# A graph attention layer: the radial network per pair of tiles on quarters of the array, one row load per pair, sums stored only where a node block ends

## The chip, the cores and the metric

One core of one Trainium2 chip runs the kernel. The metric is device time in microseconds, median of several runs. The kernel before takes 6380.22 us (three runs, 6365.9 to 6386.08).

## The reference

One attention layer over a graph of 12500 nodes with 128 features and 400000 edges, sorted by destination. Cut to what matters:

```
h       = relu(layernorm(x))
message = (h @ w_src + b_src)[src] + (h @ w_dst)[dst]
rad     = silu(silu(edge_attr @ w1 + b1) @ w2 + b2) @ w3 + b3     # 32 -> 64 -> 64 -> 128
message = message * edge_weight * rad
msg_h   = (message @ w_sep + b_sep) as 8 heads of 16 alpha + 16 value
score   = sum(smooth_leaky_relu(alpha) * alpha_dot) per head
att     = softmax of score over the edges of one dst
out     = x + segment_sum(value * att, dst) @ w_proj + b_proj
```

## The kernel before

Nodes are cut into 98 blocks of 128. Edges, in order of destination, are cut into chunks of 256. An item is a chunk with one node block that it touches; two items make a tile of 512 edges, sixteen tiles a group. There are 1664 items, 832 tiles and 52 groups. A first stage (to about 250 us) works out node features and tables, among them the rows of places (each edge's node within its block, rel_rows) and of edge weights (ea_rows). A last stage (from about 6290 us) divides and projects. The edge stage between them is written out completely: each engine has its own `step(g, j)` for tile t = 16 g + j, all in one fixed order, tied by semaphores only.

In step t:

- SP loads for tile t + 3 the transposed attributes (attr, 32 KB per item), the two windows of destination rows (win, 128 KB per item, only if the block has changed in that slot), the places (rel_bc, L986) and the edge weights (ea_bc, L987), both one row broadcast to 128 partitions. Which block an item belongs to is worked out in SP's registers from packed words (`steer_to`). Then it stores the running sums of tile t - 29 (L1005). At j = 14 it also loads the group's masks in ten transfers. Four buffers each.
- GpSimd gathers source rows, four indirect DMAs of 128 rows per tile (L1047), let go when the transposes of tile t - 4 are done.
- PE (TensorE): transposes of the gathered rows into xT_ps (L1337); z1 of tile t + 1 (L1256); the aggregation of tile t - 28 (L1297); every fourth step the scores (L1307); softmax odds and ends; then, when the message is there, alpha (a_ps, L1353), z2 of t + 1 (L1262), values (v_ps, L1358), radial of t + 1 (L1271, two row halves), destination part of t + 1 (L1284). Every f32 matmul is two instructions, an f32r one and a transpose are one.
- VectorE: message of tile t, xT_ps times rads (L1159); `weigh` of t - 27: one-hot places (hot, L1123) and weighted values (wval, L1129); `accumulate` of t - 28: two steps of the running sum with the aggregation (L1146, L1149), into one of four buffers that must have been stored; a piece of the softmax; the smooth leaky ReLU (L1169); rads of t + 1 (L1115), which reads radial's PSUM.
- ScalarE: first Silu of t + 1 (L1184), copy of the values (L1204), Silu of alpha (L1231), second Silu of t + 1 (L1190), places to a one-hot by distance (L1196, L1198) for t + 2, the copy of a tile's weights (L1211).

Radial's output takes half of each of two PSUM banks (rad_ps); the aggregation writes beside it. The softmax's small products have a bank of their own (misc_ps).

Of the kernel before, what the change touches and what calls it, by code (L numbers as in the profile page):

```python
# [4 lines left out]
P = 128  # L5
# [4 lines left out]
CE = 2 * P  # L10
TE = 2 * CE
# [3 lines left out]
LAG = 28  # L15
# [47 lines left out]
def gnn_kernel(nc, x, src, dst, edge_attr, edge_weight, w_src, b_src, w_dst, fc_w1, fc_b1, fc_w2, fc_b2,  # L63
# [32 lines left out]
    rel_rows = dram("rel_rows", (NI, CE), bf16)  # L96
    ea_rows = dram("ea_rows", (NI, CE))
# [6 lines left out]
    with ctx:  # L104
# [27 lines left out]
        z_ps = ctx.enter_context(nc.psum_tensor("z_ps", [P, 512], f32))  # L132
# [4 lines left out]
        misc_ps = ctx.enter_context(nc.psum_tensor("misc_ps", [P, 512], f32))  # L137
        rad_ps = ctx.enter_context(nc.psum_tensor("rad_ps", [P, 2, 512], f32))
        PS = [v[:, :] for v in (z_ps, xT_ps, a_ps, v_ps, sc_ps, misc_ps)] + [rad_ps[:, 0], rad_ps[:, 1]]
# [15 lines left out]
        with ExitStack() as part, nc.Block() as block:  # L155
# [10 lines left out]
            count_ps = misc_ps  # L166
# [250 lines left out]
        with ExitStack() as part, nc.Block() as block:  # L417
# [79 lines left out]
            def _(sp):  # L497
# [24 lines left out]
                def store_rows(k):  # L522
# [3 lines left out]
                    sp.dma_start(ea_rows[rows, :], ea_g[:, u]).then_inc(s_out[u], 16)  # L526
# [3 lines left out]
                    sp.dma_start(rel_rows[rows, :], rel_b[:, u]).then_inc(s_out[u], 16)  # L530
# [335 lines left out]
        with ExitStack() as part, nc.Block() as block:  # L866
# [7 lines left out]
            attr = tb("attr", [P, U, P])  # L874
            win = tb("win", [P, U, 2, PARTS, C], f32r)
            rel_bc = tb("rel_bc", [P, U, TE], bf16)
            ea_bc = tb("ea_bc", [P, U, TE])
            idx = tb("idx", [P, 2, 2 * G], i32)
            gath = tb("gath", [P, U, SUB, C])
            hotT = tb("hotT", [P, 2, TE], f32r)  # L880
            apart = tb("apart", [P, 2, TE])
            row_below = tb("row_below", [P, 1])
            h1 = tb("h1", [P, 2, CE])
            h2 = tb("h2", [P, 2, CE])
            rads = tb("rads", [P, 2, TE])
# [3 lines left out]
            hot = tb("hot", [P, 2, SUB, P])  # L889
            wval = tb("wval", [P, 2, SUB, H, HV])  # L890
# [21 lines left out]
            s_attr = [ts(f"attr_in{u}") for u in range(U)]  # L912
            s_win = [ts(f"window_in{u}") for u in range(U)]
            s_ea = [ts(f"edge_weight_in{u}") for u in range(U)]
            s_gath = [ts(f"gathered{u}") for u in range(U)]
            s_idx = [ts(f"indices_in{n}") for n in range(2)]
            s_rst = [ts(f"run_stored{r}") for r in range(R)]
# [27 lines left out]
            def _(sp):  # L945
                at = {}
                held = {}

                def steer_to(g, j):

                    half = j % (G // 2)
                    if half == 0 or j == AHEAD:
# [15 lines left out]
                def load(g, j, attr_v):  # L968
                    t = G * g + j
                    u = j % U  # L970
                    items = steer_to(g, j)
                    need(sp, s_z1, t - U + 1)
                    for i, (c, b) in enumerate(items):
                        sp.dma_start(attr[2 * RAD * i:2 * RAD * (i + 1), u], attr_v[bass.ds(c, 1)].rearrange("o f e -> (o f) e")).then_inc(s_attr[u], 16)
# [32 lines left out]
                def stepper(attr_v):  # L1007
                    def step(g, j):
                        t = G * g + j
                        if there(t + AHEAD):  # L1010
                            load(*later(g, j, AHEAD), attr_v)
# [9 lines left out]
                        if there(t - LAG - 1):  # L1021
                            store(*later(g, j, -LAG - 1))
# [535 lines left out]
```

## Time and profile before

| | |
|---|---|
| median of 3 runs | 6380.22 us |
| the profiled execution | 6405.65 us |
| its span | 6403.9 us |
| mean granted TensorE clock | 0.944 |
| PE busy | 5329.2 us, 83% |
| VectorE (DVE) busy | 3944.8 us, 62% |
| GpSimd (POOL) busy | 3635.5 us, 57% |
| ScalarE (ACT) busy | 3145.8 us, 49% |
| moved by DMA | 905.74 MB |

The profile is of one execution. Busy shares are means over stages. A matmul's end is modelled, while the moment at which an engine that waited for it starts is recorded. "remote" as a releaser is a signal that the profile gives to no instruction. PEclk is the granted clock of TensorE as a share of 2.4 GHz.

### The profile page before, as it was taken

To read this page: it belongs to the slowest core of one execution; us is meant where nothing else is said; L and a number is where in the kernel's file an instruction comes from. 1 tells how busy PE (TensorE), PEld (TensorE's weight loads), DVE (VectorE), ACT (ScalarE), POOL (GpSimd) and SP (SyncE) were. 2 spreads that over 40 slices of the span, in tenths; PEclk is the share of its full clock that TensorE was granted. 3 is DMA by queue.
4 is the path that set the end of the run, shared out by engine and by line. 5 is a ranking of instruction groups with operands and counts; after the bars stand their busy time and mean duration, and the time that the engine had idled before them with its cause. 6 is when DMAs were issued, how large, how long until landed. Compare 5 with 4: busy or idle time off the path is not lost. (4 is left out here: it accounts for less than half of the span.)

```text
span 6403.9 us, 120739 instructions
## 1 busy us (share of the span) xinstructions
PE 5329.2 (83%) x33155; PEld 4049.4 (63%) x33155; DVE 3944.8 (62%) x7812; ACT 3145.8 (49%) x6435; POOL 3635.5 (57%) x3491
## 2 busy tenths in 40 slices
PE   4678888888888888888888888888888888888886
PEld 3456666666666666666666666666666666666665
DVE  6336666666566665666656666566666666656677
ACT  3445554555455454555544545555555555554541
POOL 2455555565565565555655556565555655555535
PEclk8799999999999999999999999999999999999985
DMA  6544444444454455555555555555555555555544
GB/s 188 147 109 125 124 132 129 130 131 131 131 139 133 130 144 136 139 139 144 141 142 143 143 144 144 150 148 148 150 150 150 159 151 157 149 155 152 153 114 135
DMA packets 949500, 905.74 MB, mean 141 GB/s; under 512 B 174324, under 2 KB 784408, under 8 KB 948511
## 3 DMA queue, kind: packets, MB, share of 16 engines
q1 hardware_dynamic: 818491, 659.02, 36.6%
q0 software_dynamic: 108784, 223.44, 13.7%
q10 hardware_dynamic: 21556, 15.50, 0.9%
q8 instruction: 281, 4.60, 0.3%
q14 instruction: 388, 3.18, 0.2%
HBM read 863.59 MB, written 152.34 MB: 159 GB/s over the span
## 5 line engine op out<-in xcount | busy, mean ns | idle before, releaser
L1047 POOL DMA_INDIRECT gath<-msg_src,idx x3328 | 3492.4, 1049 | 2473.6 <-issue 1040.9
L1353 PE MATMUL a_ps<-msgT,wa 128*128 128x512 f32 x1664 | 932.4, 642 | 367.1 <-DVE msgT L1159 362.3
L1184 ACT ACTIVATE h<-z_ps,b 128x256 f32<-128x256 f32 x832 | 394.7, 474 | 1683.2 <-PE z_ps L1256 1012.5
L1159 DVE TENSOR_TENSOR msgT<-xT_ps,rads 128x512 f32<-128x512 f32 x832 | 575.4, 692 | 1048.8 <-remote 729.6
L1231 ACT ACTIVATE sil<-a_ps,ba 128x512 f32<-128x512 f32 x832 | 573.5, 689 | 1169.4 <-PE a_ps L1353 638.5
L1297 PE MATMUL rad_ps<-wval,hot 128*128 128x136 f32 x6656 | 987.3, 294 | 140.3 <-DVE rads L1115 102.3
L1297 PEld LDWEIGHTS rad_ps<-wval,hot 128*128 128x128 f32 x6656 | 887.2, 201 | 178.9 <-DVE rads L1115 128.4
L1115 DVE SCALAR_TENSOR_TENSOR rads<-rad_ps,b,ea_bc 128x512 f32<-128x512 f32 x832 | 622.6, 748 | 587.9 <-PE rad_ps L1271 333.7
L1358 PEld LDWEIGHTS v_ps<-wv,msgT 128*128 128x128 f32 x6656 | 874.5, 193 | 59.8 <-ACT vals L1204 12.8
L1358 PE MATMUL v_ps<-wv,msgT 128*128 128x128 f32 x6656 | 891.1, 277 | 0.0
L1271 PE MATMUL rad_ps<-h,w 64*128 64x256 f32 x3328 | 609.7, 444 | 337.0 <-ACT h L1190 237.1
L1169 DVE SCALAR_TENSOR_TENSOR sil<-a_ps,sil 128x512 f32<-128x512 f32 x832 | 569.1, 684 | 325.8 <-ACT sil L1231 177.8
L1284 PEld LDWEIGHTS xT_ps<-hotT,win 128*128 128x128 f32 x3328 | 467.9, 197 | 291.8 <-issue 291.8
L1353 PEld LDWEIGHTS a_ps<-msgT,wa 128*128 128x128 f32 x1664 | 253.0, 191 | 621.7 <-DVE msgT L1159 550.4
L1284 PE MATMUL xT_ps<-hotT,win 128*128 128x256 f32 x3328 | 645.6, 318 | 0.1
L1262 PEld LDWEIGHTS z_ps<-h,w 128*128 128x128 f32 x1664 | 310.8, 192 | 482.9 <-issue 426.7
L1196 ACT ACTIVATE apart<-rel_bc,row_below 128x512 f32<-128x512 bf16 x832 | 599.1, 720 | 5.0 <-DMA rel_bc<-rel_rows 5.0
L1129 DVE TENSOR_TENSOR wval<-vals,wT 128x512 f32<-128x512 f32 x832 | 569.3, 684 | 0.0
L1123 DVE TENSOR_TENSOR hot<-iota_row,rel_tab 128x512 f32<-128x512 f32 x832 | 566.7, 681 | 0.0
L1256 PE MATMUL z_ps<-attr,w 128*128 128x128 f32 x3328 | 535.3, 286 | 19.1 <-DMA attr<-in_edge_attr_t 19.1
L1262 PE MATMUL z_ps<-h,w 128*128 128x256 f32 x1664 | 511.0, 389 | 45.7 <-issue 33.4
L1271 PEld LDWEIGHTS rad_ps<-h,w 64*128 64x128 f32 x3328 | 259.7, 191 | 446.7 <-ACT h L1190 248.0
(233 smaller groups left out, 5744.9 us busy)
## 6 DMA issues: line engine op xcount, KB each, us to landing
win<-msg_dst SPq DMA_DIRECT2D x1664, 128.0 KB
ea_bc<-ea_rows SPq DMA_DIRECT2D x832, 256.0 KB
sums<-run SPq DMA_DIRECT2D x832, 136.0 KB
rel_bc<-rel_rows SPq DMA_DIRECT2D x832, 128.0 KB
attr<-in_edge_attr_t SPq DMA_DIRECT2D x1664, 32.0 KB
gath<-msg_src,idx POOLq DMA_INDIRECT x3328
msg_dst<-dst_parts SPq DMA_DIRECT2D x98, 128.0 KB, 1.8
pen_g<-pen_rows SPq DMA_DIRECT2D x208, 32.1 KB
```

The costliest lines, as they stand in the source:

```text
L1047: pool.indirect_dma_start(gath[:, u, s], None, msg_src, bass.IndirectOffsetOnAxis(ap=idx[:, j // 8, at:at + 1], axis=0)).then_inc(s_gath[u ...
L1115: dve.scalar_tensor_tensor(rads[:, j % 2].rearrange("p (i e) -> p i e", i=2), rad_ps[:, :, 0:CE], b3[:, :], ea_bc[:, j % U].rearrange("p ( ...
L1129: dve.tensor_tensor(wval[:, u, :, :, 0:AH], vals[:, bass.ds(G * (g % 2) + j, 1)].rearrange("p o s (h k) -> p (o s) h k", h=H), wT[:, :, at ...
L1159: dve.tensor_tensor(msgT[:, q], xT_ps[:, :], rads[:, q], ALU.mult).then_inc(s_msg, 1)
L1196: act.activation(apart[:, j % 2], rel_bc[:, j % U], ACT.Square, bias=row_below[:, :]).then_inc(s_apart, 1)
L1231: act.activation(sil[:, j % 8], a_ps[:, :], ACT.Silu, bias=ba[:, :]).then_inc(s_sil, 1)
L1262: pe.matmul(z_ps[:, 0:CE], lhsT=w2[:, :], rhs=h1[:, j % 2], start=True, stop=True).then_inc(s_z2, 1)
L1271: last = pe.matmul(rad_ps[:, i, 0:CE], lhsT=w3[rows, :], rhs=h2[rows, j % 2], start=True, stop=True, tile_position=(FC * i, 0))
L1284: last = pe.matmul(xT_ps[:, cols], lhsT=win[:, j % U, i, n], rhs=hotT[:, j % 2, cols], start=(i == 0 and n == 0), stop=False, skip_group_c ...
L1297: last = pe.matmul(rad_ps[:, i, CE:CE + AW], lhsT=hot[:, j % 2, s], rhs=wval[:, j % 2, s].rearrange("p h k -> p (h k)"), start=(r == 0), s ...
L1353: pe.matmul(a_ps[:, :], lhsT=wa[:, :], rhs=msgT[:, q], start=True, stop=True).then_inc(s_a, 1)
L1358: last = pe.matmul(v_ps[:, s * P:(s + 1) * P], lhsT=msgT[:, q, s * P:(s + 1) * P], rhs=wv[:, :], start=True, stop=True)
```

## The change

Six things together. The radial network runs once for two tiles: z1 and z2 are four matmuls each on 64 x 64 quarters of the array, radial four of 512 columns, and its output fills both banks of rad_ps; the aggregation and the softmax's small products use the same banks after rads has been read. Tiles' elementwise steps around it (both Silus, apart, hotT, rads, hot) are one instruction per pair. Places and edge weights lie in one row (edge_rows) and come as one load per pair of tiles, in two buffers. Attributes are loaded 7 tiles ahead in eight buffers. Running sums are stored per pair, and only if one of its items is its block's last, or the pair is every fourth, or it lies at the very end. The lag goes from 28 to 30 tiles, and the softmax's pieces move to other steps. The bank of misc_ps becomes a second bank of z_ps.

```diff
-LAG = 28
+LAG = 30
-                    sp.dma_start(ea_rows[rows, :], ea_g[:, u]).then_inc(s_out[u], 16)
+                    sp.dma_start(edge_rows[rows, REL_W:ROW_W], ea_g[:, u]).then_inc(s_out[u], 16)
...
-                    sp.dma_start(rel_rows[rows, :], rel_b[:, u]).then_inc(s_out[u], 16)
+                    sp.dma_start(edge_rows[rows, 0:REL_W], rel_b[:, u].bitcast(f32)).then_inc(s_out[u], 16)
...
+            UA = 8
+            AHEAD_A = UA - 1
+            rows_bc = tb("rows_bc", [P, 2, 4, ROW_W])
...
-                    need(sp, s_rads, t - U + 1)
-                    need(sp, s_hotT, t - U + 1)
-                    sp.dma_start(rel_bc[:, u], edges(rel_rows)[bass.ds(t, 1), :].broadcast_to((P, TE))).then_inc(s_win[u], 16)
-                    sp.dma_start(ea_bc[:, u], edges(ea_rows)[bass.ds(t, 1), :].broadcast_to((P, TE))).then_inc(s_ea[u], 16)
+                    if t % 2 == 0:
+                        k = t // 2
+                        need(sp, s_rads, k - 1)
+                        need(sp, s_hotT, k - 1)
+                        sp.dma_start(rows_bc[:, k % 2].rearrange("p i w -> p (i w)"),
+                                     edge_rows.rearrange("(k i) w -> k (i w)", i=4)[bass.ds(k, 1), :].broadcast_to((P, 4 * ROW_W))).then_inc(s_rows[k % 2], 16)
...
                 def store(g, j):
+                    k = (G * g + j) // 2
+                    h = k % 4
...
+                    sp.wait_ge(s_run, 4 * k + 4)
...
+                    if h == 3 or k >= LAST // 4:
+                        sp.dma_start(rows, pair).then_inc(s_rst[k % 2], 16)
+                    else:
+                        ends_here = (at["stored"] // 2 ** (4 * h)) % 16
+                        sp.dma_start(rows, pair, cond=(ends_here != 0)).then_inc(s_rst[k % 2], 16)
...
                 def scale_rad(g, j):
+                    dve.scalar_tensor_tensor(rads[:, j % 4:j % 4 + 2].rearrange("p n (i e) -> p (n i) e", i=2),
+                                             rad_ps[:, :, :].rearrange("p n (i e) -> p (n i) e", i=2), b3[:, :],
+                                             rows_bc[:, k % 2, :, REL_W:ROW_W], ALU.add, ALU.mult).then_inc(s_rads, 1)
...
                 def step(g, j):                                      # VectorE
+                    if there(t - LAG):
+                        accumulate(*later(g, j, -LAG))
+                    if j % 2 == 0:
+                        if there(t + 2 - LAG):
+                            mark(*later(g, j, 2 - LAG))
+                    elif there(t + 1 - LAG):
+                        weigh(*later(g, j, 1 - LAG))
...
-                        if there(t + 1):
+                        if j % 2 and there(t + 1):
                             scale_rad(*later(g, j, 1))
...
+                def z1(k):                                           # PE
+                    for i in range(2):
+                        for r in range(2):
+                            last = pe.matmul(z_ps[FC * r:FC * (r + 1), i, 0:CE], lhsT=w1[rows, r, rows],
+                                             rhs=attr[rows, 2 * u:2 * u + 2].rearrange("p n e -> p (n e)"), start=True, stop=True,
+                                             tile_position=(FC * i, FC * r))
+                def z2(k):
...
+                def radial(k):
+                            last = pe.matmul(rad_ps[cols, n, :], lhsT=w3[rows, cols], rhs=h2[rows].rearrange("p i r e -> p (i r e)"), start=True, stop=True,
+                                             tile_position=(FC * n, FC * q))
...
                         last.then_inc(s_xT, 1)
-                        if there(t + 1):
-                            z1(*later(g, j, 1))
+                        pe.wait_ge(s_rads, t // 2 + 1)
...
+                        if q:
+                            k = t // 2
+                            need(pe, s_run, 2 * (t - LAG) + 2)
+                            if k + 1 < NPAIR:
+                                radial(k + 1)
+                            if k + 2 < NPAIR:
+                                z2(k + 2)
+                            if k + 3 < NPAIR:
+                                z1(k + 3)
                         if there(t + 1):
-                            radial(*later(g, j, 1))
                             dst_part(*later(g, j, 1))
```

## Rows read from the trace of the kernel before

**Rows 1.** The page's first part: busy us, share of the span, instructions.
```profile
PE 5329.2 (83%) x33155; PEld 4049.4 (63%) x33155; DVE 3944.8 (62%) x7812; ACT 3145.8 (49%) x6435; POOL 3635.5 (57%) x3491
```

**Rows 2.** The message's line: whole run, 280 to 400 us, 3000 to 4000 us.
```profile
L1159 DVE TENSOR_TENSOR msgT<-xT_ps,rads x832: 690/692/694, 252.8 to 6193.5; 128x512 f32<-128x512 f32 x167
...
L1159 DVE TENSOR_TENSOR msgT<-xT_ps,rads x18: 690/692/693, 279.5 to 396.5; 128x512 f32<-128x512 f32 x18
```

**Rows 3.** Busy us by engine in three stretches, clock, DMA share, GB/s.
```profile
280.00:400.00 120.00, 96.61 (x524) 68.57 (x524) 40.24 (x57) 58.44 (x107) 66.71 (x70) 0.90 0.43 116
3000.00:4000.00 1000.00, 857.79 (x5425) 649.77 (x5423) 622.53 (x1171) 511.15 (x1023) 589.53 (x559) 0.97 0.52 143
6193.00:6290.00 97.00, 63.93 (x270) 53.98 (x267) 64.69 (x143) 10.91 (x34) 0.00 (x0) 0.57 0.18 53
```

**Rows 4.** Groups by line: busy us, mean ns of one, idle before it.
```profile
L1047 POOL DMA_INDIRECT gath<-msg_src,idx x3328 | 3492.4, 1049 | 2473.6 <-issue 1040.9
...
L1297 PE MATMUL rad_ps<-wval,hot 128*128 128x136 f32 x6656 | 987.3, 294 | 140.3 <-DVE rads L1115 102.3
```

**Rows 5.** One step in order of time: start, length, instruction, idle before.
```profile
4878.12 0.69 DVE L1159 TENSOR_TENSOR msgT<-xT_ps,rads 128x512 f32<-128x512 f32 x1 [1.67 <-remote]
...
4878.86 1.13 PE L1353 MATMUL a_ps<-msgT,wa 128*128 128x512 f32 x2 [0.62 <-DVE msgT L1159]
4878.87 1.36 POOL L1047 DMA_INDIRECT gath<-msg_src,idx  x1 [1.79 <-remote]
...
4879.83 0.59 PE L1262 MATMUL z_ps<-h,w 128*128 128x256 f32 x2
...
4880.26 1.05 PE L1358 MATMUL v_ps<-wv,msgT 128*128 128x128 f32 x8
...
4881.24 0.70 PE L1271 MATMUL rad_ps<-h,w 64*128 64x256 f32 x4
...
4881.88 0.75 PE L1284 MATMUL xT_ps<-hotT,win 128*128 128x256 f32 x4
4881.99 0.75 DVE L1115 SCALAR_TENSOR_TENSOR rads<-rad_ps,b,ea_bc 128x512 f32<-128x512 f32 x1 [0.31 <-issue]
...
4882.46 0.60 PE L1337 MATMUL xT_ps<-ident,gath 128*128 128x128 f32 x4
...
4883.03 0.94 POOL L1047 DMA_INDIRECT gath<-msg_src,idx  x1 [0.30 <-issue]
...
4884.88 0.69 DVE L1159 TENSOR_TENSOR msgT<-xT_ps,rads 128x512 f32<-128x512 f32 x1 [2.14 <-remote]
```

**Rows 6.** Who waited for whom: total us, times, longest.
```profile
SPq L1005 <- DVE run L1149: 540.8, 484, 5.1
...
DVE run L1146 <- remote: 280.8, 100, 6.2
```

**Rows 7.** Groups by line: the scores on four strips, and alpha.
```profile
L1307 PE MATMUL sc_ps<-sil,adot 128*32 128x512 f32 x1664 | 224.7, 612 | 0.0
L1353 PE MATMUL a_ps<-msgT,wa 128*128 128x512 f32 x1664 | 932.4, 642 | 367.1 <-DVE msgT L1159 362.3
```

**Rows 8.** DMA issues of one kind: issuer, count, size.
```profile
sums<-run SPq DMA_DIRECT2D x832, 136.0 KB
```

**Rows 9.** In order of time: accumulation in a step with mask loads.
```profile
3915.47 0.35 DVE L1146 SCALAR_TENSOR_TENSOR run<-run,keep,rad_ps 128x136 f32<-128x136 f32 x1 [3.91 <-remote]
```

**Rows 10.** In order of time, tiles 20 and 21: messages, gather, ScalarE's Silu.
```profile
396.55 0.69 DVE L1159 TENSOR_TENSOR msgT<-xT_ps,rads 128x512 f32<-128x512 f32 x1
...
401.66 0.69 DVE L1159 TENSOR_TENSOR msgT<-xT_ps,rads 128x512 f32<-128x512 f32 x1 [0.49 <-PE xT_ps L1337]
...
406.92 0.95 POOL L1047 DMA_INDIRECT gath<-msg_src,idx  x1 [0.30 <-issue]
...
409.89 0.69 ACT L1231 ACTIVATE sil<-a_ps,ba 128x512 f32<-128x512 f32 x1 [5.07 <-remote]
...
414.26 0.69 DVE L1159 TENSOR_TENSOR msgT<-xT_ps,rads 128x512 f32<-128x512 f32 x1 [1.24 <-PE xT_ps L1337]
```

More of the change, by code:

```diff
@@ L10 @@
 CE = 2 * P
+REL_W = CE // 2
+ROW_W = REL_W + CE
 TE = 2 * CE
@@ L1024, in stepper @@
                         sp.dma_start(idx[:, half], idx_rows[half]).then_inc(s_idx[half], 16)
-                    for j in range(AHEAD):
-                        load(0, j, attr_v)
+                    for j in range(AHEAD_A):
+                        load_attr(0, j, attr_v)
+                        if j < AHEAD:
+                            load(0, j)
                     stream(sp, step)
@@ L1250, in _ @@
             def _(pe):
-                def z1(g, j):
-                    t = G * g + j
-                    pe.wait_ge(s_attr[j % U], 32 * (4 * g + j // U) + 32)
-                    need(pe, s_h2, t)
-                    for r in range(2):
-                        last = pe.matmul(z_ps[:, r * P:(r + 1) * P], lhsT=w1[:, r], rhs=attr[:, j % U], start=True, stop=True)
-                    last.then_inc(s_z1, 1)
-                def z2(g, j):
-                    t = G * g + j
-                    pe.wait_ge(s_h1, t + 1)
-                    pe.matmul(z_ps[:, 0:CE], lhsT=w2[:, :], rhs=h1[:, j % 2], start=True, stop=True).then_inc(s_z2, 1)
@@ new lines, in z2 @@
+                def z2(k):
+                    pe.wait_ge(s_h1, k + 1)
+                    need(pe, s_h2, k)
+                    for r in range(2):
+                        rows = slice(FC * r, FC * (r + 1))
+                        for n in range(2):
+                            last = pe.matmul(z_ps[FC * n:FC * (n + 1), r, CE:2 * CE], lhsT=w2[rows, rows], rhs=h1[rows, :, n, :], start=True, stop=True,
+                                             tile_position=(FC * r, FC * n))
+                    last.then_inc(s_z2, 1)
@@ new lines, in radial @@
+                def radial(k):
+                    pe.wait_ge(s_h2, k + 1)
+                    need(pe, s_rads, k)
+                    for n in range(2):
+                        rows = slice(FC * n, FC * (n + 1))
+                        for q in range(2):
+                            cols = slice(FC * q, FC * (q + 1))
+                            last = pe.matmul(rad_ps[cols, n, :], lhsT=w3[rows, cols], rhs=h2[rows].rearrange("p i r e -> p (i r e)"), start=True, stop=True,
+                                             tile_position=(FC * n, FC * q))
```

291 lines of the change are left out of this document (156 added, 135 removed).

## The prediction

> **What bounds the kernel now.** I read the page's first two parts first. PE is busy 83% of the span at nearly full granted clock, no other engine over 62% [rows 1]. A reader would call it PE-bound. The windows and the message product (line 1159, one per tile of 512 edges) ask for care: its 832 instructions start from 252.8 to 6193.5 us, so the edge stage gives 5940.7/832 = 7.14 us a tile, and the other 463 us are outside it [rows 2]. From 3000 to 4000 us PE is busy 857.8 of 1000 us, 6.1 of 7.14 us a tile, so 1.0 us a tile is idle [rows 3].
>
> Next, what PE's idle time costs. Tiles 1 to 18 have no aggregation yet (it lags by 28 tiles). There 18 messages fall into 120 us, 6.67 us a tile [rows 2], though PE has the 987.3/832 = 1.19 us of line 1297 less to do a tile [rows 4] and is busy only 96.6 of 120 us [rows 3]. So 1.19 us less PE work, and the VectorE work that goes with it, bought 0.47 us: 0.40 us a us. PE's load matters, but a loop through several engines sets the step.
>
> One step in order of time shows that loop [rows 5]. Message at 4878.12; alpha product 4878.86; z2 4879.83; values 4880.26; radial 4881.24; destination part 4881.88; transposes 4882.46 to 4883.06; next message only at 4884.88, 6.76 us after the first. 1.8 us of this are a wait for the transposes' signal, which comes long after their recorded end (matmul ends are modelled). The other member of the loop is GpSimd: four gathers a tile, let go by the transposes, from 4878.87 to 4883.97. They need (3492.4 + 1040.9)/832 = 5.45 us a tile [rows 4], the floor below every change that leaves them as they are.
>
> SP is a third thing close by: its longest wait in the stage, for the sums to store, is 540.8 us, 0.65 us a tile [rows 6], so it works up to 6.5 us a tile.
>
> **The change, part by part.**
>
> *Radial network.* Before, start to start on PE [rows 5]: z2 0.43, radial 0.64; z1 has z2's columns in smaller pieces, 0.43 too. That is 1.50 us a tile, 3.00 a pair. After, per pair: z1 four quarter matmuls of 256 columns, z2 the same, radial four of 512. If the four run side by side, a group lasts as long as one full-array matmul of its length: z1 and z2 0.43 each, radial the alpha product's 0.97 (4878.86 to 4879.83). Sum 1.83, saved 1.17 us a pair, 0.59 us a tile. That quarters overlap isn't in the trace; the nearest row is the score matmul on four column strips: 1664 instructions of 512 columns busy 224.7 us, against 932.4 us for 1664 of the same length on the whole array, 4.1 times less [rows 7]. I take full overlap; the other end is pairs of quarters only, 3.66 us a pair, 0.33 us a tile more than now.
>
> The Trainium skill ("TensorE: Matmul & The Clock Gate", Part 3, measured speedup) gives four row tiles of 512 columns 3.07 times, not 4. The strips of this trace gave 4.1. By the page the 7.32 us of serial quarters would take 2.38 us, a saving of 0.31 us a tile instead of 0.59, and the forecast would be about 93 us later.
>
> How much of the 0.59 arrives? Two ends. As a PE-bound stage: 0.59 x 832 = 491 us. By the loop alone: the even step loses z2 and radial (-1.07 us); the odd step's radial grows by 0.33 and z1 moves ahead of its transposes (+0.43), +0.76; together -0.31 a pair, 129 us. The slope of 0.40 lies between: 0.59 x 0.40 x 832 = 196 us. I take 196.
>
> *Elementwise work in pairs.* rads, hot, both Silus, apart and hotT become one instruction of double length per pair. That saves fixed parts on VectorE and ScalarE, which are 62% and 49% busy [rows 1] and wait in every step: counted as nothing. The cost is lateness: the double rads ends later after the odd step's radial product. In the step shown rads ends at 4882.74 and the message starts at 4884.88 [rows 5], so 2.1 us cover the extra 0.75 at most; without that cover it would be 416 x 0.75 = 312 us. PE's new wait for rads ahead of the aggregation (the bank is shared now) has z2, z1, the destination part and the transposes between as cover. The weights' transposes, moved to the values' bank, make the values of one step in 16 wait for ScalarE's copy: 0 to 52 x 2 us, and I take 0, since the step has idle time of that size.
>
> *Row load.* The same bytes, as one transfer per pair with 6 KB a partition. Per pair SP issues 1 instead of 4. Attribute loads, 32 KB, just go 7 tiles ahead instead of 3, past the window loads. Store issues halve, and a conditional one adds register work. SP has 14 issues a pair now (4 attributes, 4 windows, 4 rows, 2 stores) and 10 after: its 6.5 us lie between 6.5 x 10/14 = 4.6 and, if the conditions cost what the issues save, 6.5, under the step forecast here (6.75): nothing on the path, though at 6.5 hardly any cover is left. The one load brings tile t+3 no later than now in program order, with two pair buffers where four were; 0 taken, at most one landing of some us a stall.
>
> *Stores.* Now 832 of 136 KB, 113 MB [rows 8]. After: every fourth pair, 104, and those in which one of 98 node blocks ends, at most some 74 more, of 272 KB: some 48 MB. Accumulation (line 1146) waits 280.8 us in 100 places for something that is no engine's [rows 6]; it waits for the aggregation's signal and for a store to have landed four tiles back. At 3915.47 it starts after 3.91 us of such a wait, in a step in which SP loads the masks [rows 9]. Bounds: 0 and 281 us. I take 130, nearly half, because PE's own signals are late in the same places. The store that must have landed is now two to three steps back; a late one costs as before.
>
> *Lag 30.* Two more draining steps: the 97 us after the last message hold some 28 [rows 3], 3.4 us each: +7.
>
> Sum against the profiled execution: 6405.65 - 196 - 130 + 7 = 6087. The median shown is 25 us under that execution (6380.22), so 6062.
>
> **Rivals.**
>
> *PE is the bound after all* (17%): all 491 us arrive, 6405.65 - 491 - 130 + 7 - 25 = 5767. For it: 83% busy [rows 1]. Against it: the 18 tiles without aggregation.
>
> *Gathers run into each other; slower* (23%). Where the transposes' signal comes before the running four gathers end, the next four follow without a gap, and in the trace PE's signals then come late: messages at 396.55, 401.66 and 414.26, eight gathers in one row up to 407.87, ScalarE idle 5.07 us and let go at 409.89, 2.0 us after the last gather [rows 10]. Two steps took 17.71 us instead of 14.28, +3.43. The even step, 1.07 us shorter up to its transposes, ends them some 3.1 us after the first gather's start (4883.06 - 1.07 - 4878.87), inside the third gather. So every pair is a candidate. The gain of 319 us is gone at 93 such pairs more than now out of 416; at 200 it is 6062 + 686 = 6748. Against it: the odd step is longer, and less DMA traffic may shorten the gathers' tail.
>
> *The gather loop holds the step* (12%): 5.10 us of gathers, 0.75 to their start, 0.9 to the late signal make 6.8 us [rows 5] whatever PE does; only part of the store waits goes: 6250 to 6387, say 6340.
>
> *Quarters overlap only in twos* (6%): +0.33 x 0.40 x 832 = 110 us, and up to 275 if PE bounds, the store waits apart: 6362 to 6527, say 6450. The change wouldn't do what it says.
>
> **How the numbers follow.** The forecast has 42%. Its own range: the loop end (129) with no store gain, 6259; the PE half-way (350) with 281, 5757: 5880 to 6260 allowing both not to fall together. The range with the rivals, 5740 to 6650, leaves out some 2 in 10, nearly all in the gathers' rival and below PE's. Within 0.3% (19 us, about what can be told from no change here): 0.01 of the forecast, half of the loop rival, a little of the gathers' one: 0.08. Faster: 0.41 + 0.17 + 0.05 = 0.63. Slower: 0.22 + 0.06 + 0.01 = 0.29.
>
> **What would show it.** Starts of line 1159's successor: a mean of 6.75 us a tile in the forecast, even steps shorter than odd. z1, z2 and radial together about 1.8 us of PE start to start a pair; 3.7 means no overlap. Accumulation's waits well under 280 us. Wrong: gathers in rows of eight with PE signals after them, a step held at 6.8, ScalarE or VectorE waiting for the row load, or SP never waiting.

## The result, and the profile after

The changed kernel takes 6399.14 us (median of 13 runs, 6370.56 to 6423.66), the one before 6375.61 beside it (13 runs, 6350.9 to 6387.24): a ratio of 1.0043 with the 95% interval [1.0027, 1.0059]. The forecast was 6062 us. The predicted direction was wrong, and the time lies inside the range.

The record does not name the chip of this comparison. In the last six experiments, on two chips (6 and 4), the kernel before took 5245 us, and on chip 4 the changed one took 4911 beside it: a ratio of 0.9366 [0.9353, 0.9379]. Both results are real; most of what follows is about what lies between them.

The page's first part after, as [rows 1]:
```profile
PE 5062.4 (79%) x34819; PEld 3516.6 (55%) x34819; DVE 3864.9 (60%) x6980; ACT 2823.2 (44%) x4771; POOL 3595.7 (56%) x3491
```
The message's line (now L1193), as the whole run in [rows 2], and the three stretches of [rows 3], with the same columns:
```profile
L1193 DVE TENSOR_TENSOR msgT<-xT_ps,rads x832: 674/692/693, 272.8 to 6178.2; 128x512 f32<-128x512 f32 x167
```
```profile
280.00:400.00 120.00, 87.48 (x559) 56.04 (x560) 37.55 (x46) 50.55 (x71) 67.43 (x71) 0.86 0.38 118
3000.00:4000.00 1000.00, 811.47 (x5687) 561.07 (x5685) 606.02 (x1031) 456.75 (x742) 576.82 (x557) 0.92 0.42 130
6193.00:6290.00 97.00, 49.32 (x223) 44.51 (x223) 55.10 (x121) 7.01 (x27) 0.00 (x0) 0.64 0.17 50
```
The edge stage from first to last message went from 5940.7 to 5905.4 us, 35 less. The first message came 20.0 us later, and what follows the last one (span less its start) grew from 210.4 to 222.3 us. 35.3 - 20.0 - 11.9 = 3.4 us, the difference of the spans (6403.9 and 6400.5). PE was busy 267 us less and stood idle for nearly all of that time.

Where it stood idle is told by who waited, and for what (engine, line, releaser: total us, times, longest). After, against [rows 6] for the accumulation:
```profile
ACT h L1228 <- remote: 953.8, 258, 6.8
DVE rads L1140 <- remote: 626.8, 200, 7.0
ACT vals L1244 <- remote: 408.2, 140, 6.6
ACT sil L1277 <- remote: 333.7, 74, 7.5
DVE run L1181 <- remote: 307.2, 99, 6.7
DVE msgT L1193 <- remote: 163.4, 97, 4.6
```
Each of these instructions waits for a signal of PE (the accumulation for a landed store too), and the signal came so long after the recorded end of PE's work that the profile gives it to no instruction. (Matmul ends are modelled, so the trace does not tell whether the product itself was late or only its signal; "held" below means either.) All such waits of VectorE, ScalarE and PE together are 2857 us after; before they are 2179, the message's 729.6 the largest. One pair of tiles after, in order of time:
```profile
3008.03 0.69 DVE L1193 TENSOR_TENSOR msgT<-xT_ps,rads 128x512 f32<-128x512 f32 x1 [0.40 <-PE xT_ps L1394]
...
3011.75 0.94 POOL L1072 DMA_INDIRECT gath<-msg_src,idx  x1 [2.04 <-issue]
...
3012.77 0.69 DVE L1193 TENSOR_TENSOR msgT<-xT_ps,rads 128x512 f32<-128x512 f32 x1 [0.31 <-PE xT_ps L1394]
3013.00 0.95 POOL L1072 DMA_INDIRECT gath<-msg_src,idx  x1 [0.30 <-PE xT_ps L1394]
...
3014.48 1.05 PE L1417 MATMUL v_ps<-wv,msgT 128*128 128x128 f32 x8
...
3015.46 1.09 PE L1325 MATMUL rad_ps<-h,w 64*64 64x512 f32 x8
...
3019.07 0.28 PE L1338 MATMUL xT_ps<-hotT,win 128*128 128x256 f32 x1 [1.04 <-issue]
...
3019.54 0.94 POOL L1072 DMA_INDIRECT gath<-msg_src,idx  x1 [0.30 <-issue]
...
3019.79 0.28 PE L1338 MATMUL xT_ps<-hotT,win 128*128 128x256 f32 x1 [0.44 <-issue]
...
3020.56 0.28 PE L1338 MATMUL xT_ps<-hotT,win 128*128 128x256 f32 x1 [0.49 <-issue]
...
3022.04 0.60 ACT L1244 ACTIVATE vals<-v_ps 128x512 f32<-128x512 f32 x1 [5.22 <-remote]
3022.13 1.28 DVE L1140 SCALAR_TENSOR_TENSOR rads<-rad_ps,b,rows_bc 128x1024 f32<-128x1024 f32 x1 [4.51 <-remote]
...
3023.51 0.69 DVE L1193 TENSOR_TENSOR msgT<-xT_ps,rads 128x512 f32<-128x512 f32 x1
```
The even step, without radial work, is short: 4.74 us. Its transposes let the next four gathers go while the last four are still under way, so that seven gathers, from 3011.75 to 3020.48, follow each other with the 0.30 us between two that the gathers of a row have here. The values and the radial product were done by about 3015.5 and 3016.5, but ScalarE and VectorE learn of it at 3022.04 and 3022.13. The odd step takes 10.74 us.

Such a pair is no more than one half of the picture. I took every pair of tiles of the stage but the first and the last, and asked whether four gathers that begin in it follow the last four within 0.35 us (a "row of eight"). The mean step from the even tile's message, from the odd tile's, and the sum, in us:

| pairs | number | even | odd | sum |
|---|---|---|---|---|
| after, with such a row | 204 | 4.49 | 9.91 | 14.40 |
| after, without | 210 | 6.83 | 7.22 | 14.05 |
| before, with such a row | 47 | 7.69 | 9.32 | 17.01 |
| before, without | 367 | 7.27 | 6.65 | 13.92 |

In the changed kernel a row moves time from the even step to the odd one and adds only 0.35 us to the pair. The pairs without one are not shorter than those of before either, though PE has less to do in them. In these pairs the four gathers last 5.0 to 5.2 us, and the next message comes 1.3 us after the last of them at the median; before, 1.0. The gathers and the late signal behind them set the step.

A stretch of the same length on chip 4 (the changed kernel, unedited):
```profile
3009.65 1.05 PE L1417 MATMUL v_ps<-wv,msgT 128*128 128x128 f32 x8
...
3010.63 1.09 PE L1325 MATMUL rad_ps<-h,w 64*64 64x512 f32 x8
3010.74 0.60 ACT L1244 ACTIVATE vals<-v_ps 128x512 f32<-128x512 f32 x1 [0.20 <-PE v_ps L1417]
...
3011.34 0.94 POOL L1072 DMA_INDIRECT gath<-msg_src,idx  x1 [0.31 <-issue]
3011.54 0.61 PE L1314 MATMUL z_ps<-h,w 64*64 64x256 f32 x8
...
3011.79 1.28 DVE L1140 SCALAR_TENSOR_TENSOR rads<-rad_ps,b,rows_bc 128x1024 f32<-128x1024 f32 x1 [0.37 <-PE rad_ps L1325]
3011.97 0.61 PE L1303 MATMUL z_ps<-attr,w 64*64 64x256 f32 x8
...
3012.51 0.74 PE L1338 MATMUL xT_ps<-hotT,win 128*128 128x256 f32 x4
```
There the gathers run just as closely, and the signals come at once.

### The profile page after: what moved, and what is told of

Same layout as the page of the kernel before. It is cut to its first block and busy times, and to the rows that moved or that the text cites. A ratio compares the mean times of both kernels' runs of the same rounds, so it can differ in the third digit from the quotient of the medians.

```text
span 6400.5 us, 119284 instructions
## 1 busy us (share of the span) xinstructions
PE 5062.4 (79%) x34819; PEld 3516.6 (55%) x34819; DVE 3864.9 (60%) x6980; ACT 2823.2 (44%) x4771; POOL 3595.7 (56%) x3491
## 2 busy tenths in 40 slices
DMA packets 633218, 836.99 MB, mean 131 GB/s; under 512 B 143764, under 2 KB 521400, under 8 KB 632255
## 5 line engine op out<-in xcount | busy, mean ns | idle before, releaser
L1072 POOL DMA_INDIRECT gath<-msg_src,idx x3328 | 3453.4, 1038 | 2492.9 <-issue 1177.4
L1351 PE MATMUL rad_ps<-wval,hot 128*128 128x136 f32 x6656 | 1075.1, 311 | 355.1 <-DVE rads L1140 229.1
L1140 DVE SCALAR_TENSOR_TENSOR rads<-rad_ps,b,rows_bc 128x1024 f32<-128x1024 f32 x416 | 533.5, 1282 | 791.8 <-remote 626.8
L1193 DVE TENSOR_TENSOR msgT<-xT_ps,rads 128x512 f32<-128x512 f32 x832 | 574.3, 690 | 552.4 <-PE xT_ps L1394 360.8
L1228 ACT ACTIVATE h<-z_ps,b 128x512 f32<-128x512 f32 x416 | 285.7, 687 | 1043.0 <-remote 953.8
L1244 ACT ACTIVATE vals<-v_ps 128x512 f32<-128x512 f32 x832 | 488.9, 588 | 492.0 <-remote 408.2
L1181 DVE SCALAR_TENSOR_TENSOR run<-run,keep,rad_ps 128x136 f32<-128x136 f32 x780 | 275.1, 353 | 643.1 <-remote 307.2
L1325 PE MATMUL rad_ps<-h,w 64*64 64x512 f32 x3328 | 482.3, 651 | 200.0 <-DVE run L1184 91.8
L1394 PE MATMUL xT_ps<-ident,gath 128*128 128x128 f32 x3328 | 532.8, 278 | 96.2 <-issue 96.0
L1149 DVE TENSOR_TENSOR hot<-iota_row,rel_tab 128x1024 f32<-128x1024 f32 x416 | 506.9, 1219 | 0.0
L1234 ACT ACTIVATE apart<-rows_bc,row_below 128x1024 f32<-128x1024 bf16 x416 | 474.4, 1140 | 0.0
L1394 PEld LDWEIGHTS xT_ps<-ident,gath 128*128 128x128 f32 x3328 | 396.6, 143 | 121.4 <-issue 121.3
```

The lines of the kernel that those rows point to most:

```text
L1072: pool.indirect_dma_start(gath[:, u, s], None, msg_src, bass.IndirectOffsetOnAxis(ap=idx[:, j // 8, at:at + 1], axis=0)).then_inc(s_gath[u ...
L1140: dve.scalar_tensor_tensor(rads[:, j % 4:j % 4 + 2].rearrange("p n (i e) -> p (n i) e", i=2), rad_ps[:, :, :].rearrange("p n (i e) -> p (n ...
L1149: dve.tensor_tensor(hot[:, u:u + 2].rearrange("p n s q -> p (n s) q"), iota_row[:, :].unsqueeze(1).broadcast_to((P, 2 * SUB, P)), rel_tab[ ...
L1193: dve.tensor_tensor(msgT[:, j % 2], xT_ps[:, :], rads[:, j % 4], ALU.mult).then_inc(s_msg, 1)
L1351: last = pe.matmul(rad_ps[:, j % 2, AW * i:AW * (i + 1)], lhsT=hot[:, j % 4, s], rhs=wval[:, j % 4, s].rearrange("p h k -> p (h k)"), star ...
L1394: last = pe.matmul(xT_ps[:, s * P:(s + 1) * P], lhsT=gath[:, j % U, s], rhs=ident[:, :], is_transpose=True, start=False, stop=True, skip_g ...
```

## The experiments

The experiments were made in five groups, each on one chip beside the kernel before: e1 to e4 (chip 0), e5 to e8 (3), e9 to e12 (1), e13 to e16 (6), e17 and e18 (4). On the first three chips before takes 6326 to 6357 us, on the last two 5245. Only ratios within a group are compared, unless said. e1, e2, e3 and e9 load other rows than the edges ask for, so they compute other values: they leave the choice of rows out. "Step" is the mean distance of messages; "held" is the sum of the waits for remote, GpSimd's left out.

| run | us | before beside it | ratio | step | held |
|---|---|---|---|---|---|
| before, first profile | | | | 7.15 | 2179 |
| after, first profile | 6399 | 6376 | 1.004 | 7.11 | 2857 |
| e1 after, plain loads, ScalarE | 4918 | 6334 | 0.776 | 5.34 | 1 |
| e2 before, plain loads, ScalarE | 5436 | 6334 | 0.858 | 5.99 | 6 |
| e3 after, plain loads, GpSimd | 4910 | 6334 | 0.775 | 5.32 | 2 |
| e9 after, two of four gathers | 4915 | 6357 | 0.773 | 5.33 | 13 |
| e4 after, gathers in twos | 6267 | 6334 | 0.991 | 6.95 | 2982 |
| e10 after, one by one | 6094 | 6357 | 0.959 | 6.70 | 2158 |
| e11 before, in twos | 6186 | 6357 | 0.974 | 6.85 | 2053 |
| e7 after, in eights | 7785 | 6326 | 1.230 | 8.76 | 5249 |
| e5 after, await message | 6692 | 6326 | 1.059 | 7.46 | 3448 |
| e6 before, await message | 6917 | 6326 | 1.094 | 7.75 | 2558 |
| e8 before, conditional stores | 6422 | 6326 | 1.014 | 7.17 | 1854 |
| e12 after, all stores, in twos | 6303 | 6357 | 0.992 | 7.00 | 3055 |
| e17 after, unedited | 4911 | 5245 | 0.937 | 5.33 | 0 |
| e18, e15 after, one by one b | 4912, 4914 | 5245 | 0.937 | 5.33 | 0 |
| e16 before, one by one b | 5245 | 5245 | 1.000 | 5.76 | 0 |
| e13 after, short pauses | 5148 | 5245 | 0.982 | 5.61 | 0 |
| e14 after, long pauses | 5641 | 5245 | 1.076 | 6.21 | 0 |

### Is it the gathers?

```diff
-                        pool.indirect_dma_start(gath[:, u, s], None, msg_src, ...idx...).then_inc(s_gath[u], 16)
+                        first_row = TE * j + P * s          # e3, from GpSimd; e1, e2: act.dma_start, three tiles ahead
+                        pool.dma_start(gath[:, u, s], msg_src[first_row:first_row + P, :]).then_inc(s_gath[u], 16)
```
e1: 

> The kernel after, with each tile's four indirect gathers (GpSimd's queue) replaced by four plain loads of 128 consecutive rows of the same table into the same buffers, issued by ScalarE three tiles ahead; the rows are not those of the edges, so the values differ from the reference. Theory A (TensorE's signals that fall due under a tile's gathers come about 0.9 us after the last of them, and a step that is short pushes two chains of gathers together, so that the next is long): without gathers on GpSimd the even and odd steps lose their long cases; mean step 6.0 to 6.4 us instead of 7.11, time 5480 to 5850 us. Theory B (the pair's own order costs it: the radial batch of 1.9 us in every second step, with ScalarE's and VectorE's pair operations behind it): the mean step stays at 6.9 to 7.1 us, time 6200 to 6400 us. Theory C (only the late start, 20 us, and the tail, 12 us, took the gain, and the step is PE's): step 7.0 to 7.1 us, time 6350 to 6400.

e2: 

> The kernel before with the same edit: plain loads of 128 consecutive rows from ScalarE's queue for the four gathers, other values. Theory A: the step of before is held at 6.8 us by the gathers' loop, so this one falls too, less than the kernel after does, since TensorE has 0.59 us a tile more to do: mean step 6.4 to 6.8 us against 7.15, time 5800 to 6100 us, and the changed kernel under plain loads is faster than this one by 3 to 8%. Theory B: this one keeps its time within 1% and stays at or below the changed kernel with plain loads. Theory C: both kernels keep their times within 1%.

e3: 

> The kernel after with the four gathers replaced by four plain loads of the same rows as in the first run, but issued from GpSimd's queue at the place and under the wait of the gathers; other values. It tells the work of GpSimd for a gather from the traffic. If it is the 1.04 us of descriptor work on GpSimd for each gather that holds TensorE's signals, then a plain load, where GpSimd is as long in it, keeps 6350 to 6450 us, and where it is short (under 0.3 us) it falls to the time of the first run. If it is only the scattered rows in memory, this falls to the first run's time however long GpSimd is in it.

All three fell far below what even theory A had allowed, and every remote wait went with the gathers, but for 1 to 6 us. (e2 took 5436 us, where before takes 5245 with its gathers on chips 6 and 4. That ScalarE's issues lie in its way is argued, not shown. The two kernels with plain loads are 4918/5436 = 0.905 apart.) Theories B and C are out: the pair's order stands in all of e1 and e3. e3 moves the same packets and bytes on GpSimd's queue as the gathers do, GpSimd is in each load 537 ns, and nothing is held. So neither the number of bytes and packets nor the queue is enough to hold signals. The indirect form, its 1038 ns on GpSimd, or the rows scattered over the table (e3 reads 128 in a row) does it; which of the three, no run tells. GpSimd's row of e3, then of after:
```profile
L1073 POOL DMA_DIRECT2D gath<-msg_src x3328 | 1764.1, 537 | 2691.3 <-PE xT_ps L1394 2094.1 <-issue 567.0 <-DMA idx<-idx_rows 29.5
```
```profile
L1072 POOL DMA_INDIRECT gath<-msg_src,idx x3328 | 3453.4, 1038 | 2492.9 <-issue 1177.4
```
e9 keeps the first two gathers of a tile and makes the other two plain:

> The kernel after with a tile's first two loads still indirect gathers and its last two plain loads of 128 consecutive rows, all from GpSimd's queue; half of the gathered rows are other rows. All four gathers indirect: 6399 us; none: 4910 us. Theory A, as the runs so far have shaped it (TensorE's signals are held from the third gather of a chain on, until about 0.9 us after its last one): chains of two gathers hold nearly nothing, so most of the 1490 us goes: 4950 to 5300 us. If instead each gather holds the same, 5600 to 5750 us. Above 6000 us neither would be right.

4915 us, below either range: two gathers a tile cost nothing, four some 1480 us (6399 - 4915, on different chips; the ratios are 1.004 and 0.773). The hold is not a price per gather.

### How do the gathers have to lie?

```diff
                     for s in range(SUB):
+                        if s == 2:                              # e4, e11: in twos
+                            need(pool, s_v, t - U + 1)
```
```diff
+                        if s == 1: need(pool, s_agg, t - U - LAG + 1)    # e10: one by one
+                        elif s == 2: need(pool, s_v, t - U + 1)          # (b, e15, e16, e18: s_a)
+                        elif s == 3: need(pool, s_D, t - U + 2)          # (b: s_v, t - U + 1)
```
```diff
-                    need(pool, s_xT, t - U + 1)
+                    if j % 2 == 0:                              # e7: in eights
+                        need(pool, s_xT, t - U + 2)
```
```diff
-                    need(pool, s_xT, t - U + 1)
+                    need(pool, s_msg, t - U + 1)                # e5, e6
```
e4: 

> The kernel after, with one wait added on GpSimd: the third and fourth gather of a tile start only once the values of the tile whose buffer they fill are projected (the signal after the message), so that chains of more than four gathers can't form. Theory A: the back-to-back chains (208 of 832 tiles after, 51 before) go to nearly none; at 3.43 us for each chain removed and some new holds behind shorter chains, 6000 to 6250 us. Theory B and C: the time stays within 0.5% of 6399 or grows by the wait.

e7: 

> The kernel after, where GpSimd waits for TensorE's transposes only once in two tiles, for both buffers, and then issues eight gathers one behind the other (8.9 to 10 us of a pair's 14.2). Theory A1: signals are held under eight gathers, for all of the chain or for its last: if for all of it, two long steps in every pair and 6800 to 7500 us; if only under the last gather of a chain, one hold for two tiles in place of two and 5800 to 6300 us. Theory A2: as the latter. Theory B: 6399 within 1%.

e10: 

> The kernel after with each of a tile's four gathers behind a wait of its own: the transposes of the tile whose buffer is filled, then the aggregation, the values and the destination rows of that step. GpSimd has 4 x 1.05 = 4.2 us of gathers in a step in any case. If the hold needs a chain of three or more gathers, 5500 to 6000 us; if the backlog of gathers (about 1.25 us each by the hold's end behind fours and eights) is what counts, however they are spaced, 6100 to 6400 us.

e11: 

> The kernel before with one wait added: a tile's third and fourth gather wait for the values of the tile whose buffer they fill, as in the fourth run. There the kernel after fell from 6399 to 6267 us. Theory A: the step of before (6.8 us, a loop of wait 0.77, gathers 5.1, hold 0.9) is no longer one chain, and falls to 6.3 to 6.7 us: 5900 to 6200 us. If twos only cured the collisions of the changed kernel, of which before has few (51 of 832 tiles), this one stays at 6300 to 6400 us.

e5: 

> The kernel after with one word changed: before a tile's four gathers GpSimd waits for VectorE's message signal of the tile whose buffer they fill, where it waited for TensorE's signal of that tile's transposes; the gathers start about 0.9 us later. Theory A1 (TensorE's signals are held while gathers run, whatever GpSimd waits for next): the waits put down to remote on VectorE and ScalarE (2625 us together after, 0 with plain loads) stay within a quarter, time 6300 to 6450 us. Theory A2 (it is GpSimd's wait on a signal of TensorE, standing behind the last gather of a chain, that holds TensorE's signals): with no such wait left the remote waits fall below a quarter of that and the time comes near the plain loads', 4950 to 5500 us. Theory B, already weakened by the plain loads: 6399 us.

e6: 

> The kernel before with the same one word changed. Theory A1: 6.8 us become 0.77 later start plus the rest of the loop, so the step grows by up to 0.9 us or stays: 6300 to 6900 us. Theory A2: 5450 to 5800 us.

e4 missed its range by 17 us: 42 rows of eight and more were left (182 in the unedited kernel), but 202 of six had come, since a wait that is already met parts nothing. In e10 too only 303 gathers stand alone; 237 rows still have four. e11 met its range at the edge. e7 took longer than either case said, e10 lies between its two, and e5 and e6 lie above those of theory A1, by 242 and 17 us. Still they end theory A2: with no wait of GpSimd on a signal of PE left, more is held, not less. They also speak for the loop. A tile's first gather began 0.75 us after the message's start and begins 1.48 us after it now (medians, in both kernels), and the steps grew by 0.36 and 0.61 us (7.46 - 7.11; 7.75 - 7.15), as they would with the gathers' start on the path; but e6 also has 129 rows of eight and more, where before had 24.

With the same two waits in both kernels the changed one is the slower: 0.991 of before (e4) against 0.974 (e11), on different chips. Where signals are held, nothing here shows that the change itself gains: before with gathers one by one was not run on such a chip.

The forms order themselves by how long gathers go without a pause: eights 1.230, fours 1.004, twos 0.991, one by one 0.959, and in before fours 1, twos 0.974. To see it in the single signal, count in the traces the messages for which VectorE had nothing else to do when their transposes ended, by what GpSimd was doing at that moment. In the kernel before, of 376 whose transposes ended in the fourth gather of a row, 93 of 100 came over 0.5 us late, by 1.80 us at the median; of 117 that met GpSimd idle, 15 of 100. In e11 it is 16 of 100 in a second gather (217 messages), 95 in a fourth (244). In e7 all of the 173 in or just behind the fourth or fifth of eight were late, by 6.4 to 6.7 us at the median, and none of the 341 that met GpSimd idle. The message then comes some 0.9 us after a row's last gather behind fours, 1.7 behind eights. Over the ten traces of these chips with four indirect gathers a tile, 91 of 100 were late when the gather two before the latest one had begun 2.5 to 3.0 us earlier (1119 messages), 6 of 100 when that was over 4 us (2200).

Only PE's signals come late. In the trace of before, its first and last 400 us left out, of 739 Silus of ScalarE that waited for PE's z1 or z2, 69 of 100 began over 0.5 us after its recorded end. Of 386 alpha products of PE that waited for VectorE's message none did (0.06 us at the most), nor any of 333 leaky ReLUs of VectorE that waited for ScalarE's Silu (0.46 at the most).

That the density is the cause, not only its companion, was to be shown with pauses:

```diff
+                        need(pool, s_idle, SUB * t + s)
+                        pool.memset(idle[:, 0:128], 0.0).then_inc(s_idle, 1)   # e13; 320 numbers in e14
```
e13: 

> The kernel after, with a memset of 128 numbers on one partition (an estimate of 0.2 us from the profile's memsets of GpSimd: 1.05 us for 1152 numbers, 0.1 for one) put on GpSimd ahead of every gather; it writes a tile that nobody reads. Gathers then begin about 1.5 us apart in place of 1.25, so the second one back began 3.0 us before. If the density of gathers is what holds TensorE's signals, the waits put down to remote fall by more than half and the time falls to 5500 to 6000 us, though GpSimd does more. If any chain of gathers holds signals until its end, chains are now 6.0 us long, and the step grows to 7.7 us or more: 6600 to 7000 us.

e14: 

> The same with memsets of 320 numbers (an estimate of 0.4 us): gathers begin about 1.7 us apart, four of them 6.8 us. Density: nearly no holds are left, and GpSimd's own 6.8 us a tile sets the step: 832 x 6.8 plus 490 us ahead and behind, 6100 to 6200 us. Chain: 6900 us or more.

e15: 

> The kernel after with each gather of a tile behind its own wait, for the transposes, the aggregation, the alpha input and the values of the step that frees its buffer (the run before with the aggregation, the values and the destination rows took 6094 us). These four signals lie more evenly in a step (about 0, 1.5, 2.6, 3.7 us after the transposes against 0, 1.5, 3.7, 4.5). Density: fewer triples of gathers within 3 us, 5900 to 6090 us. Otherwise 6094 us within 1%.

e16: 

> The kernel before with the same four waits (its run with twos took 6186 us against 6357). Density: 6000 to 6150 us. If the changed kernel's shorter TensorE work counts where holds are fewer, this one is slower than the changed kernel with the same waits by 1 to 4%; if the collisions of the changed kernel still eat it, the two are within 1%.

Without the kernel before beside them these four would have looked like large gains. It took 5245 us there, and nothing was held in any of them, so they say nothing on density. What they do show is GpSimd's own loop: in e13 a gather, a memset and the gaps take (3493.2 + 646.9 + 549.2 + 31.6)/832 = 5.67 us a tile, and the step is 5.61. (The gaps at the stage's edges are in the sum.) e16 against before, 0.9999 [0.9989, 1.0008], shows that the four waits themselves cost nothing there, and lets its trace stand for before on such a chip. Before with these waits is 6.7% slower than the changed kernel with them (5245 against 4914), more than the 1 to 4% expected with holds.

e17: 

> The changed kernel as it is, nothing edited, beside the kernel before on the same chip. If the kernel before takes some 5245 us there (no holds), the changed one takes 4910 to 4960 us, 0.937 to 0.946 of it: the four waits then did nothing, and the forecast's saving of TensorE arrives. If the kernel before takes some 6350 us (holds), it takes 6370 to 6420 as it did.

e18: 

> The kernel with each gather behind its own wait (transposes, aggregation, alpha input, values) once more. Without holds 4914 us, within 0.5% of the changed kernel. With holds it takes 5900 to 6100 us, 0.93 to 0.96 of the kernel before, as the run with the other four waits did (6094).

4910.8 and 4911.9 us: the first case of both expectations. The changed kernel with every gather takes there what e1, e3 and e9 take without them on the other chips. The message's line of e17 and its waits have no remote left:
```profile
L1193 DVE TENSOR_TENSOR msgT<-xT_ps,rads x832: 677/691/694, 257.1 to 4688.4; 128x512 f32<-128x512 f32 x167
its engine sat idle before it (us, times) until:
  PE xT_ps L1394: 293.8, 577
  issue: 1.1, 2
```
and of e16, for before:
```profile
L1165 DVE TENSOR_TENSOR msgT<-xT_ps,rads x832: 690/692/693, 246.2 to 5035.3; 128x512 f32<-128x512 f32 x167
its engine sat idle before it (us, times) until:
  PE xT_ps L1343: 274.0, 806
  DVE rads L1121: 5.2, 15
  issue: 3.2, 10
```
3000 to 4000 us in e16, then in e17 (columns as in [rows 3]):
```profile
3000.00:4000.00 1000.00, 995.27 (x6698) 770.56 (x6698) 769.41 (x1451) 630.82 (x1266) 714.15 (x692) 1.00 0.66 183
```
```profile
3000.00:4000.00 1000.00, 969.74 (x7619) 696.13 (x7619) 808.72 (x1378) 612.24 (x993) 772.31 (x748) 1.00 0.60 186
```
Without holds before is bound by PE, busy 995 of 1000 us at the full clock, 2.4 GHz; after, PE is busy 970. Per tile that is 5.74 and 5.17 us of PE, so 0.57 us was spared where 0.59 was forecast. GpSimd hardly waits in e17 either; its pauses that the profile gives to no releaser are 0.3 us at the longest:
```profile
POOL gath L1072 <- issue: 940.0, 3084, 0.3
```
Its last 3312 gathers are one row: 1.030 us and a pause of 0.305, four times, make 5.34 us a tile, the step itself (5.33). e3, where GpSimd waits for the transposes in most steps, has the same step, so PE and its waits for the message set it; GpSimd has nothing left beside it.

### The stores

e8 puts the condition on each tile's store in the kernel before. e12 takes the conditions out of the changed kernel, with gathers in twos.
```diff
-                        sp.dma_start(rows, pair, cond=(ends_here != 0)).then_inc(s_rst[k % 2], 16)
+                        sp.dma_start(rows, pair).then_inc(s_rst[k % 2], 16)
```
e8: 

> The kernel before with the conditional stores alone: a tile's sums (136 KB) go out only where one of its two items ends a node block or is the last of its group of eight tiles. The forecast gave the waits of the accumulation 0 to 281 us, taken as 130. If stores free the buffers sooner, VectorE's remote waits at the accumulation (280.8 us) go and the time falls by 0 to 130 us; if those waits are the same held TensorE signals as at the message, they stay and the time is 6335 within 0.5%.

e12: 

> The kernel after with gathers in twos and every pair's sums stored without a condition. The conditional stores alone made the kernel before 1.4% slower, where the forecast had 0 to 2.0% faster. If that holds in the changed kernel, 6267 us fall by 50 to 100 us: 6170 to 6220. If it came from the store for each tile and SyncE's arithmetic for each, which the pairs halve, 6250 to 6290 us.

Neither expectation of e8 held: the conditions made before slower, 1.0142 [1.0096, 1.0188]. The accumulation's waits stayed:
```profile
DVE run L1154 <- remote: 216.1, 96, 7.2
```
In the changed kernel they make no difference: 0.992 against the 0.991 of e4, on another chip; e12's 6303 us lie 13 us above the second of its ranges. Why before lost 95 us stays open. Its steps of over 8.5 us went from 80 to 97, which would fit a shift in how signals meet gathers; that is argued and not shown.

## Why the prediction was wrong, step by step

*What bounds the kernel.* The loop was seen right: 6.8 us from gathers' start through a late signal [rows 5]. Its third member, the "late signal", was taken as a property of the step. Three chips had it and two had not; e16 is the same work at 5.76 us a step, PE-bound. One trace could not tell.

*Radial network.* Right. In the pair shown for e17, radial starts at 3010.63, z2 at 3011.54, z1 at 3011.97 and the destination part at 3012.51: 1.88 us (the median of 414 pairs too), against 1.83 forecast, and 3.00 before. Full overlap holds, quarters in twos (3.66) are out. By the Trainium skill ("TensorE: Matmul & The Clock Gate", Part 3, measured speedup), 3.07 times for four row tiles, an estimate was 2.38 us: this trace's quarters do better, as its strips did.

*How much of the 0.59 us arrives: the step that failed.* The forecast let 0.40 of PE's saving reach the time, 196 us. Where signals are held nothing of it arrives: pairs of tiles without a row of eight take 14.05 us after and 13.92 before, and the whole stage fell by 35 us. The path is the gathers, 5.1 us from the first one's start to the last one's end, and the late signal behind them, and neither got shorter; PE's saving turned into waiting. That the forecast had seen this path [rows 5] and priced it at 0.40 is the error. The slope was misread besides: the messages at 279.5 and 396.5 [rows 2] are 17 steps apart, 6.88 us a step and not 120/18 = 6.67. So 1.19 us less PE work had bought 0.26 us, a slope of 0.22, and the term would have been 108 us. Even that mixes PE's work with VectorE's, and with holds that fall where they fall in 17 steps.

Where nothing is held the stage went from 4789.1 (e16) to 4431.3 us (e17): 358 us, 0.43 a tile, 0.73 of what PE was spared. The rest, 133 us, is about what PE waits for the message in e17 (134.2 us) and did not before (5.8 in e16).

*The gather loop holds the step* (12%, 6340) is the rival that comes nearest on the chips with holds; its 6340 us are within 1% of the 6399 measured. Starting the gathers later lengthens the step (e5, e6), and spreading them shortens it, from 7.11 us to 6.95 and 6.70 (e4, e10) and in before from 7.15 to 6.85 (e11).

*Gathers run into each other* (23%) came true in place and signs, not in price. Four gathers that follow the last four within 0.35 us: 51 of 832 before, 208 after. Even-to-odd and odd-to-even steps are 5.7 and 8.6 us (before 7.3 and 7.0). 157 more rows are more than the 93 of the break-even, and the expected 6748 us did not come. The price of 3.43 us from the one place in [rows 10] fits the kernel before, where a pair with a row is 3.1 us longer (17.01 - 13.92). After, it is 0.35 us longer (14.40 - 14.05), about 70 us for the 204 pairs (an estimate), since the even step there is short and the odd one long. This compares pairs as they fell; no run took the rows out and left all else.

*PE is the bound* (17%, 5767) is what chips 6 and 4 show, at 4911 us.

*Quarters overlap only in twos* (6%) is out, as said; its 6362 and 6527 leave the 7 us of the lag out of the sum.

*Stores, 130 us.* Wrong in the term, right in a bound (0). The accumulation waits 307.2 us after against 280.8 [rows 6], and without holds for nothing remote: these were held signals of the same kind, or at least went with them. That the bytes fell was right: 905.74 to 836.99 MB in all, 69 less, where 65 were forecast from [rows 8].

*Elementwise pairs, 0, and row load, 0.* Right in the steps, as far as e17 shows: it has no wait for the row load, no message there waits for rads, and SP still waits for PE (612.2 us at the windows' line). Missed at the stage's start: the first message came 20.0 us later, 10.9 without holds, where VectorE waits 21.3 us at the longest for a radial product; I take that for the first pair's, which must be there in full.

*Lag 30, +7.* What lies behind the last message grew by 11.9 and 8.5 us.

Sum of the misses, in the profiled executions: forecast -319 us; measured -35 in the stage, +32 at its ends, -3.

## What to carry to other kernels

Before costing a change by a signal that comes late, ask what holds it and whether the hold is in the trace of every chip: time the kernel before beside every experiment, since here it alone took 6376 us or 5245, and e13 to e16 would have been read as gains of their edits. If a loop through another engine sets the step (here 5.1 us of gathers and the late signal behind them), count work taken off PE as nothing until the loop is opened. Price a collision from several places, and look at the whole pair: a short step that is followed by a long one gains nothing. The version to try is the changed kernel with a wait ahead of each gather: 0.959 of before where signals are held (e10), and nothing lost where they are not (e18, with two of the waits on other signals). That one form was not run on both kinds of chip, nor before with it where signals are held.

## What the hardware showed

- On chips 0, 1 and 3, signals of PE are held while GpSimd works through a row of indirect gathers: two gathers in a tile's step hold 13 us in a run (e9), four 2857 us, at a cost of some 1480 us. Plain loads from the same queue held 2 us (e3). VectorE's and ScalarE's signals were on time (counted in before's trace). On chips 6 and 4 nothing was held with gathers back to back for the whole stage. Gathers last the same on both kinds (1038 and 1030 ns), so their length doesn't warn. The three groups of runs in which the kernel before has holds came before the two in which it has none, so whether it is the chip or the hour is open, and so is what in the chip makes the difference.
- In the stretch shown, PE began a matmul only every 0.7 us while signals were held. That isn't what holds them: of some 22500 distances between neighbouring small matmuls in the trace after, 78 are of 0.6 to 0.85 us, in e7, which has the most held, 9, and in before none. The granted clock was lower over the runs with holds, 0.905 of 2.4 GHz on average after and 0.976 in e17, but e11 has holds at 0.966.
- Four gathers on GpSimd need 4 x (1.030 + 0.305) = 5.34 us a tile without holds, the changed kernel's step. The next saving on PE alone would bring nothing there: e13's pauses, 0.19 us a gather, took the step to 5.61.
